# A recurrent layer's output stage on pairs of tiles with gate and inner rows computed transposed, with a new order in the linear attention and a ring of three banks in the second attention

## The reference, cut to what matters

```python
# recurrent layer, behind the scan (H = 8 heads of 128); o is the scan's output, h the normalised row
gate = (h @ Wg).reshape(b, s, H, DV)                  # Wg 256 x 1024
o = rms_norm(o) * o_norm_w * silu(gate)               # per head
x = x + o.reshape(b, s, H * DV) @ Wo                  # Wo 1024 x 256
m = rms_norm(x)
y = square(relu(m @ W_fc)) @ W_proj                   # 256 x 1024, 1024 x 256
return x + y
# linear attention (16 heads of 16)
q_prime = relu(layernorm(q @ wq)) + 1e-6
z = 1.0 / (einsum(q_prime, k_prime.sum) + 1e-6)
att = einsum(q_prime, kv, z)                          # kv = k_prime^T v, once for each of 4 contexts
out = layernorm(att.reshape(...) @ dense_w + dense_b)
# self attention of the last layer: softmax over 1024 keys, 16 heads of 16
attn = softmax(q @ k^T / sqrt(DH)) @ v
```

## Time and profile before

| what | us |
|---|---|
| median of 3 runs | 6552.33 |
| lowest and highest | 6550.13, 6559.78 |
| the profiled execution: its own time | 6533.35 |
| its span | 6531.6 |
| output stage, 3499.7 to 4180.4 of the span | 680.7 |
| linear attention, 4180.4 to 4482.3 | 301.9 |
| second attention, 4628.5 to 5585.0 | 956.5 |

### The profile page before, as it was taken

The page is one execution under the profiler, slowest core; times in us unless marked ns, Lnnn a source line. Parts: engine busy times, 40 slices in busy tenths (PEclk is TensorE's granted clock), DMA queues, the critical chain, the costliest instruction groups (busy, mean ns, idle before and its releaser), DMA issues. The chain is left out here.

```text
span 6531.6 us, 143828 instructions
## 1 busy us (share of the span) xinstructions
PE 5530.0 (85%) x53632; PEld 3266.4 (50%) x53632; DVE 4018.2 (62%) x7302; ACT 3197.3 (49%) x4813; POOL 2323.1 (36%) x1900
## 2 busy tenths in 40 slices
PE   7788888887977996998897888778798999799998
PEld 3455555555854445777775555453222222344444
DVE  5999999997976554444443444356777777233333
ACT  5899999996556552222222333243355555211111
POOL 1887877885654333444442111143100000000000
PEclk8999999999989997999998999897899999899999
DMA  6111020201112333333332111144322221200000
GB/s 171 28 30 36 22 41 15 44 12 40 47 51 75 151 145 120 106 106 103 106 103 70 39 39 39 34 102 131 84 36 39 39 37 28 63 19 19 19 19 11
DMA packets 416489, 395.37 MB, mean 61 GB/s; under 512 B 232034, under 2 KB 370648, under 8 KB 407760
## 3 DMA queue, kind: packets, MB, share of 16 engines
q1 hardware_dynamic: 402128, 362.74, 20.0%
q10 hardware_dynamic: 13824, 25.17, 1.1%
HBM read 247.57 MB, written 140.23 MB: 59 GB/s over the span
## 5 line engine op out<-in xcount | busy, mean ns | idle before, releaser
L538 POOL TENSOR_SCALAR attn_u<-attn_rel,attn_aux 128x1024 f32<-128x1024 f32 x512 | 1089.1, 2127 | 270.7 <-DVE attn_nm L565 269.4
L689 PE MATMUL attn_tp<-attn_ident,attn_pr 128*128 128x128 f32 x4096 | 573.2, 284 | 241.5 <-ACT attn_pt L628 239.3
L3186 DVE TENSOR_REDUCE attn_mx<-attn_mp 128x1 f32<-128x512 f32 x1024 | 639.6, 682 | 195.7 <-PE attn_mp L3275 193.5
L3257 ACT ACTIVATE attn_pt<-attn_st 128x1024 f32<-128x1024 f32 x512 | 509.1, 1022 | 409.0 <-PE attn_st L3285 408.5
L557 DVE SCALAR_TENSOR_TENSOR attn_u<-attn_rel,attn_aux,attn_u 128x1024 f32<-128x1024 f32 x512 | 681.2, 1331 | 29.5 <-POOL attn_u L538 21.0
L689 PEld LDWEIGHTS attn_tp<-attn_ident,attn_pr 128*128 128x128 f32 x4096 | 449.7, 143 | 462.4 <-ACT attn_pt L628 323.1
L565 DVE CUSTOM_DVE_ANT_0 attn_pr<-attn_u,attn_s 128x1024 f32<-128x1024 f32 x512 | 618.4, 1208 | 45.5 <-PE attn_s L680 32.5
L649 ACT ACTIVATE attn_pr<-attn_pr,attn_nm 128x1024 f32<-128x1024 f32 x512 | 602.9, 1177 | 88.3 <-DVE attn_nm L565 88.1
L628 ACT ACTIVATE attn_pt<-attn_tp 128x512 f32<-128x512 f32 x1024 | 566.0, 621 | 11.1 <-PE attn_tp L689 5.6
L3275 PE MATMUL attn_mp<-attn_kt,attn_qt 96*128 96x512 bf16 x1024 | 371.9, 396 | 97.3 <-DVE attn_mx L3186 56.2
L3655 PE MATMUL moe_ps<-moe_w,moe_hidt 128*128 128x512 f32 x1024 | 453.2, 593 | 0.0
(11 more groups left out here) (492 smaller groups left out, 10548.8 us busy)
## 6 DMA issues: line engine op xcount, KB each, us to landing
s_qkv<-gin_qkv SPq DMA_DIRECT2D x32, 1536.0 KB, 5.1
core_qk<-s_qkv SPq DMA_DIRECT2D x32, 1024.0 KB, 5.1
attn_qt<-s_q SPq DMA_DIRECT2D x384, 64.0 KB, 2.9
attn_kt<-s_k SPq DMA_DIRECT2D x192, 128.0 KB, 4.3
core_arow<-s_alr SPq DMA_DIRECT2D x32, 512.0 KB, 3.8
core_grow<-s_gar SPq DMA_DIRECT2D x32, 512.0 KB, 3.7
core_vv<-s_qkv SPq DMA_DIRECT2D x32, 512.0 KB, 3.6
s_o<-core_o ACTq DMA_DIRECT2D x32, 512.0 KB, 2.9
```

The source lines that it names most:

```text
L538: pool.tensor_scalar(u[:, x % 4], rel[:, z % 2, 1], aux[:, s, 4 + NH + h:5 + NH + h], aux[:, s, 4 + 2 * NH + h:5 + 2 * NH + h], ALU.mult, ...
L689: ins = pe.transpose(tp[k][:, n], pr[:, x % BUF, (4 * k + n) * P:(4 * k + n + 1) * P], ident[:])
L3186: dve.reduce_max(mx[w % 2][:].rearrange("p h t a -> p (h t a)")[:, j:j + 1], mp[j % 2][:], AX.X).then_inc(m["max_done"], 1)
L3257: act.activation(pt[:, x % 4, 2 * a:2 * a + 2], st[a][:], ACT.Exp).then_inc(m["exp_done"], 1)
```

## The change

**Output stage.** The hardware loop is gone: 18 rounds are written out, and in round i PE works on pair i + 2 (turning x), pair i + 1 (gate, turning o, Wo, turning the norm) and pair i (W_fc, W_proj). The gate and inner rows are now computed transposed: the weight's 128 columns are the stationary operand, the turned x of both tiles of the pair (256 columns) is moved (`inner`), 4 quarters of 2 × 128 inner rows each, through a ring of three PSUM banks (`quarter`). So the inner rows come out as the next product wants them: their 16 turns a pair and the ACT copies behind them go, Relu is written for a quarter and squared by DVE straight into `ft` (`square`). o is normalised by one DVE multiplication per tile with the root repeated over 128 columns, turned before it is gated, and the gate, the norm's weight (now one value per partition) and the turned o in PSUM are multiplied in one DVE instruction per tile (`gate`), which replaces the ACT copy. The second norm's root is worked out on POOL from the first norm's variance (`ms`), without ACT squares. x, ident and o are loaded ahead of the weights, and each weight has its own semaphore. POOL takes powers for both tiles of a pair in one instruction.

**Linear attention.** On PE `pa` and `pt` move from the front of the step to its end; on POOL the addition to `qt` moves from the end of step s - 1 to the start of step s; on DVE den, rden and att move behind everything else, and the statistics of py ahead of y; on ACT qt and xt move ahead of at.

**Second attention.** `BODY` is 32: all steps are written out, without a loop. `mp` has three banks, used in turn by row scores, turned maxima and turned sums (`claim` waits for whoever had the bank three turns ago); `tb` is gone. `score_rows` issues one at a time: two stand on either side of each `st`. DVE only copies the turned maxima out of PSUM (`nf`); the split is done by POOL.

The row scores mp (the first of the group of two belongs to the slot before) now lie around st and op instead of in pairs behind st. The core of the diff:

```diff
-        gate, ff = r.sb("gate", [P, 2, GD]), r.sb("ff", [P, 2, FF])
-        ot, ft = r.sb("ot", [P, 2, GD]), r.sb("ft", [P, 2, FF])
-        ps = [r.ps(f"ps{z}", [P, 2, 512]) for z in range(2)]
-        ta, tb = [[r.ps(f"t{n}{z}", [P, 2, D]) for z in range(2)] for n in "ab"]
...
+        gt, ft = [r.sb(n, [P, 2, GH, 2, P]) for n in ("gt", "ft")]
+        ot, rl = r.sb("ot", [P, 2, 2, GH, P]), r.sb("rl", [P, 2, 4 * P])
+        quarter = [r.ps(f"quarter{n}", [P, 2, 2 * P]) for n in range(3)]
+        turned = r.ps("turned", [P, GH, P])
+        small = r.ps("small", [P, 2, KD, P])
+        rows = [r.ps(f"rows{z}", [P, 512]) for z in range(2)]
...
+                def gate(p, z):
+                    dve.wait_ge(m["ot_mm"], 2 * p + z + 1)
+                    dve.wait_ge(m["g_c"], 4 * p + 4)
+                    if p == 0:
+                        dve.wait_ge(m["onw_in"], 16)
+                    need(dve, "wo_mm", 2 * (p - 2) + z + 1)
+                    dve.scalar_tensor_tensor(ot[:, p % 2, z], turned[:], onw[:], gt[:, p % 2, :, z], ALU.mult, ALU.mult).then_inc(m["gated"], 1)
+
+                def square(p, q):
+                    dve.wait_ge(m["f_r"], 4 * p + q + 1)
+                    need(dve, "wp_mm", 2 * (p - 1))
+                    dve.tensor_tensor(ft[:, p % 2, 2 * q:2 * q + 2].rearrange("p k z n -> p (k z n)"), rl[:, q % 2], rl[:, q % 2], ALU.mult
+                                      ).then_inc(m["f_done"], 1)
...
+            def inner(kind, p, q, w, left, done):
+
+                number = turn[kind, p, q]
+                if number >= 3:
+                    name, value = freed[number - 3]
+                    pe.wait_ge(m[name], value)
+                for c in range(2):
+                    for k in range(KD):
+                        at = (2 * q + c) * P
+                        ins = pe.matmul(bank(kind, p, q)[:, c], w[:, k, at:at + P], left[:, p % 2, k].rearrange("p z n -> p (z n)"),
+                                        start=k == 0, stop=k == KD - 1)
+                ins.then_inc(m[done], 1)
+
...
+            for pair in rounds():
+                p2, p1, p0 = pair(2), pair(1), pair(0)
+                if p1 is not None:
+                    gates(p1)
+                    turn_heads(p1, 0)
+                if p0 is not None:
+                    hidden(p0, 0)
+                    hidden(p0, 1)
+                if p1 is not None:
+                    turn_heads(p1, 1)
+                if p0 is not None:
+                    hidden(p0, 2)
+                    hidden(p0, 3)
+                if p1 is not None:
+                    for z in range(2):
+                        mixer(p1, z)
+                if p2 is not None:
+                    turn_rows(p2)
+                if p0 is not None:
+                    for z in range(2):
+                        project(p0, z)
+                if p1 is not None:
+                    turn_norms(p1)
 
...
+                t = tile(4)
+                if t is not None:
+                    pool.wait_ge(m["qt_c"], KD * t + KD)
+                    pool.tensor_scalar(qt[:, t % 2], qt[:, t % 2], 1e-6, None, ALU.add).then_inc(m["qt_done"], 1)
...
-                t = tile(3)
-                if t is not None:
-                    pool.wait_ge(m["qt_c"], KD * t + KD)
-                    pool.tensor_scalar(qt[:, t % 2], qt[:, t % 2], 1e-6, None, ALU.add).then_inc(m["qt_done"], 1)
...
-                t = tile(4)
-                if t is not None:
-                    b = t // TPB
-                    pe.wait_ge(m["qt_done"], t + 1)
-                    pe.wait_ge(m["kvb_done"], KD * b + KD)
-                    need(pe, "att_done", t)
-                    for k in range(KD):
-                        ins = pe.matmul(pa[:, 0:NKV], qt[:, t % 2, k * P:(k + 1) * P], kvb[:, b, k], start=k == 0, stop=k == KD - 1)
-                    ins.then_inc(m["a_mm"], 1)
...
+                j = tile(TURN)
+                if j is not None:
+                    pe.wait_ge(e["a_in"][j % 4], 16 * (j // 4) + 16)
+                    need(pe, "at_c", j)
+                    transposes(pt, a[:, j % 4]).then_inc(m["at_mm"], 1)
+                t = tile(4)
+                if t is not None:
+                    b = t // TPB
+                    pe.wait_ge(m["qt_done"], t + 1)
+                    pe.wait_ge(m["kvb_done"], KD * b + KD)
+                    need(pe, "att_done", t)
+                    for k in range(KD):
+                        ins = pe.matmul(pa[:, 0:NKV], qt[:, t % 2, k * P:(k + 1) * P], kvb[:, b, k], start=k == 0, stop=k == KD - 1)
+                    ins.then_inc(m["a_mm"], 1)
                 if s in context:
...
-    BODY = 4
+    BODY = STEPS
...
-        mp = [r.ps(f"mp{n}", [P, W]) for n in range(2)]
+        mp = [r.ps(f"mp{n}", [P, W]) for n in range(3)]
         st = [r.ps(f"st{n}", [P, 2, W]) for n in range(2)]
         op = r.ps("op", [P, W])
-        tb = r.ps("tb", [P, QT, P])
...
+        def claim(eng, key):
+
+            if turn[key] >= 3:
+                name, value = free[turn[key] - 3]
+                eng.wait_ge(m[name], value)
+            return bank(key)
 
...
+            def split(it):
+                pause(pool, "nf_done", it + 1)
+                pause(pool, "nt_out", it * 16)
+                pool.tensor_copy(nt[:, 0], nf[:]).then_inc(m["n0_done"], 1)
+                pause(pool, "n0_done", it + 1)
+                pool.tensor_tensor(nr[:], nf[:], nt[:, 0], ALU.subtract).then_inc(m["nr_done"], 1)
+                pause(pool, "nr_done", it + 1)
+                pool.tensor_copy(nt[:, 1], nr[:]).then_inc(m["n1_done"], 1)
+                pause(pool, "n1_done", it + 1)
+                pool.tensor_tensor(nt[:, 2], nr[:], nt[:, 1], ALU.subtract).then_inc(m["nt_done"], 1)
...
+                            if at:
+                                score_rows(v, at[0], 4 * at[1] + 2 * a, 1)
                             score_columns(v, w, n, a)
                             if at:
-                                score_rows(v, at[0], 4 * at[1] + 2 * a)
+                                score_rows(v, at[0], 4 * at[1] + 2 * a + 1, 1)
                             if a == 0 and x >= LAG:
                                 weigh(v, x - LAG)
```

689 lines of the change are left out of this document (369 added, 320 removed).

## The result

The changed kernel takes 6174.14 us (median; 6163.67 to 6178.81), the kernel before beside it 6551.23 us (6549.64 to 6559.78). The ratio is 0.942, 95% interval 0.9403 to 0.9436: 377 us less, where 365 were forecast.

The account below looks back on a forecast made before the run. PE work, waits and low clock bound the output stage, one rs-to-rs chain the linear attention, two score banks filled in pairs the second attention. Gains 147 + 59 + 159 = 365 us: 6552.3 - 365 = 6187 us, range 6130 to 6270.

Parts of the forecast that it names:

- at the switches between turns and products: Output stage, PE: about 1.5 us a round kept beside 30.2 us of work, making rounds of 31.7 us.
- The start: Output stage: PE begins when x, o and Wg are in, 13 us with latency and queue.
- The bound of 170 for rounds without switches: Output stage: upper bound of the gain, 170 us, with rounds of 30.2 us; forecast gain 147 us.
- Loads at nothing: Output stage: doubled weight loads lie beside the product before and cost nothing; by the skill's rule 3.4 us a pair.
- the hops I added to DVE's work: Linear attention, full steps: DVE's 4.1 us becomes the bound; with hops 4.6 us a step.
- 45 with the batches: Linear attention, 23 full steps: 23 × (6.8 - 4.6) - 5 = 45 us; 5 us for four waits on batches through HBM.
- The tail: Linear attention: the 13 last steps, at half clock and bound by PE, gain 4 us.
- Rival 1: Second attention: maxima come too late, worst case 1 to 1.5 us for each of 31 steps; 6232 us; chance 0.14.
- Rivals 2 to 5: Output-stage bank hand-over 6252 us (0.07); linear attention unmoved 6242 (0.06); loads uncovered 6284 (0.03); written-out code slower than before (0.02).

Follow-up runs that it names:

- the kernel before with 22 increments: 22 semaphore increments put into DVE's program ahead of the last stage's loop, against the kernel before; 6554.47 us, ratio 1.0011.

## Why the prediction was right, point by point

**Output stage, 147 forecast, 172 in the traces.** The likeliest mechanism held: PE is the bound, the turns of ff are gone, everything else lies beside the products, and the waits with their low clock, some 7.5 us a round, are gone, as forecast. The term that was mis-sized is the 1.5 us a round "at the switches between turns and products". In the kernel before, turns and products shared banks and the next product needed the copy of the turned rows; that these hand-overs made the gaps is the likely reason. I carried them over as if they were the price of a switch. A round is the pure work of 30.2 us, measured 30.26; over fifteen rounds that is 22 of the 25 us by which the sum was off. The start was forecast at 13, the first gate product came 12.3 us into the window. The first round:

```profile
3528.28 9.46 PE L2416 MATMUL gout_quarter<-gout_xt,gout_wg 128*128 128x256 f32 x32 [0.69 <-ACT gout_xt L2398]
...
3550.79 0.63 PE L2472 MATMUL gout_small<-gout_ident,gout_mn 128*128 128x128 f32 x4 [2.30 <-DVE gout_mn L2340]
```

23 us where 25 were taken: mn waited 2.3 us and not 4; the last round took 19.6 of 20. The bound of 170 for rounds without switches was the result. Loads at nothing was right, and is now shown by their doubling.

**Linear attention, 59 forecast, 70.** Early steps 3.5 us (3.4 forecast), full ones 4.2 (4.6). The chain is cut as described, but what is next is PE and not DVE, and the hops I added to DVE's work cost nothing because DVE is not the bound. That PE is busy for only 4.1 us a step (94.37/23), where it was 5.2 before, goes with the clock, 1.00 instead of 0.86; I had not counted this. The two stretches gave 8.7 and 58.6 us against 10 and 50 (45 with the batches), the waits for the batches were four steps of 4.65 to 5.1 us, some 2.5 us in all. A further 3 us came before the first query step, where none was forecast. The tail was forecast to gain 4 and gained nothing: from the same step on it took 47.3 us before and 47.7 after. The place of y on DVE is why: with y ahead it took 44.2.

**Second attention, 159 forecast, 147.** The slot of 2.86 us came as 2.84, without waits for a bank. The step is 24.12 and not 23.6. The missing 0.5 us is PE's wait of 0.61 us for ACT's copy of the sums, in each step: I read the slot, found its waits and took them away, but never asked what ACT's order holds up once the slot is 0.7 us shorter. The experiment that moved the copy got 0.68 us a step back. The scores before the first step gave 5.3 instead of 3 us.

**The rivals.** Rival 1, the maxima too late, did not happen. The waits above, over thirty steps, hold none for the DMA of the maxima; in one step POOL's four operations ran from 4748.77 to 4750.40, the second DMA was issued at 4751.84 and landed in 2.1 us, 2.7 us before the next step's first st. DVE, at 635.58 of 723.3 us of these steps, kept up too. Rivals 2 to 5 are refuted by the bank taken away, the full steps of 4.2 us, the doubled loads, and the loop written out at no cost.

**The total.** None of the terms covered the last stage's 17 us and the delta core's 13. The first goes with the place of DVE's loop, above; that the place makes the whole 17 us is not shown. The second I can't explain, but it is not the change's doing: over fourteen traces with the same code up to there the core took 1032 to 1046 us, in the kernel before with 22 increments 1044.8. What makes before's median lie 18 us above its profiled execution no run showed either.

## What to carry to other kernels

Before you take a gap over into the forecast, ask what released it: a gap at a hand-over goes with the hand-over, it is no price of switching. When a slot gets shorter, go through every other engine's order at the rare places too (a step's first slot, the tail), since what fitted before may now be waited for. And compare untouched stages as well: two loops of unchanged code took 2 or 3% longer in kernels where more code stood ahead of them.

## What was not expected of the hardware

- What stands ahead of a loop in DVE's program moved the loop's end by 0.03 to 0.13 us in the last stage (0.69, 0.72, 0.79 and 0.82 us in four kernels with the same loop), and this went with 6 to 17 us in the 15 passes, by the length of the spells at 1.2 GHz, though kernels with the same end of 0.72 us lie up to 11 us apart.
- In the old second attention DVE stood 2.93 us at the loop's jump back instead of 0.53, and the stage took 27 us more, in the one kernel in which five packets of code were fetched in each pass; the kernel before fetched none there. This was only seen, not moved by an experiment.
- A weight load of a 128x128 block, shown with 190 ns, is hidden behind a product of 0.11 us: doubling the loads cost 7 ns each.
